# Two fused transformer layers with a 256-step recurrence: the loops over the steps written out as straight code

## What is computed

```
def step(carry, tgt):                      # 256 times, batch 4, 64 context positions
    s, c, alpha = carry
    f = conv1d(alpha, conv_w, 'SAME')      # 10 channels, 101 taps
    e = va . tanh(enc_proj + s @ Wa_s.T + f @ Wa_f.T + ba)
    alpha = softmax(where(mask, e, -1e30))
    g = sum_t alpha[t] * hbatch[t]
    y = tanh(g @ L_gy_w.T + L_gy_b + s @ L_sy.T) @ L_yy_w.T + L_yy_b
    rec = tgt @ L_ys.T + s @ L_ss.T + g @ L_gs_w.T + L_gs_b
    ig, fg, cg, og = split(rec, 4)
    c = sig(fg) * c + sig(ig) * tanh(cg)
    s = sig(og) * tanh(c)
    return (s, c, alpha), y
```

## Time and profile before

| | us |
|---|---|
| median of 3 runs | 1775.03 |
| lowest, highest | 1773.21, 1776.44 |
| profiled execution, its span from the first to the last instruction (no other time of it is listed) | 1777.0 |
| PE busy | 1506.0 |
| DVE busy | 919.2 |
| ACT busy | 528.9 |
| POOL busy | 387.5 |

### The profile page before, as it was taken

One profiled execution on the slowest core, in us unless ns is written; L12 is line 12 of the kernel. 1 busy time (PEld: TensorE's weight loads), 2 busy tenths in 40 slices (PEclk: granted clock), 3 DMA queues, 4 the chain that ended last, 5 costly groups with the idle time before them and its releaser, 6 DMA issues.

```text
span 1777.0 us, 43152 instructions
## 1 busy us (share of the span) xinstructions
PE 1506.0 (85%) x15683; PEld 1022.2 (58%) x15683; DVE 919.2 (52%) x4293; ACT 528.9 (30%) x2023; POOL 387.5 (22%) x1030
## 2 busy tenths in 40 slices
PE   6547999999888888888888888888888888887999
PEld 3334454544666666666666666666666666664443
DVE  4996643331555555555555555555555555553422
ACT  1342231221333333333333333333333333331211
POOL 3344321220000222222222222222222222222211
PEclk7658999999555555555555555555555555555999
DMA  8330000001200000000000000000000000000000
GB/s 326 141 115 11 1 1 0 1 1 52 77 0 0 0 0 0 0 0 0 0 0 0 0 0 0 0 0 0 0 0 0 0 0 0 0 0 1 1 24 25
DMA packets 17363, 34.51 MB, mean 19 GB/s; under 512 B 7476, under 2 KB 8675, under 8 KB 17332
## 3 DMA queue, kind: packets, MB, share of 16 engines
q1 hardware_dynamic: 17332, 34.10, 5.3%
HBM read 32.00 MB, written 2.10 MB: 19 GB/s over the span
## 4 chain that ended last, share of the span: by engine, by line
PE 62%; DVE 25%; issue 6%; ACT 5%; POOL 1%; DVEq 1%; SPq 1%; DMA 0%; POOLq 0%; ACTq 0%
PE bank L1243 18%; PE bank L1073 11%; PE bank L1193 6%; PE bank L1088 6%; PE bank L1221 5%; ACT eh L960 4%; DVE interT L746 4%; PE bank L1199 4%; DVE krep L764 3%; PE bank L1213 3%; DVE rinv L755 3%; DVE rs L743 2%; DVE g L760 2%; PE bank L1231 2%; DVE gat L771 2%
## 5 line engine op out<-in xcount | busy, mean ns | idle before, releaser
L1243 PE MATMUL bank<-krep,uh 128*128 128x128 f32 x1024 | 313.1, 461 | 23.6
L1243 PEld LDWEIGHTS bank<-krep,uh 128*128 128x128 f32 x1024 | 237.4, 320 | 92.4 <-DVE krep L764 92.4
L493 POOL TENSOR_TENSOR sscale<-ex,rinv 128x8 f32 x256 | 51.3, 200 | 667.6 <-DVE rinv L755 667.6
L1221 PE MATMUL bank<-eh,krep 128*128 128x4 f16 x2048 | 95.3, 168 | 92.5 <-ACT eh L960 92.5
L764 DVE TENSOR_TENSOR krep<-inv,ahn 128x128 f32<-128x128 f32 x512 | 162.2, 356 | 0.0
L1073 PE MATMUL bank<-xT,wbig 128*128 128x512 f16 x672 | 157.2, 386 | 3.7 <-DVE xT L591 3.7
L743 DVE TENSOR_TENSOR rs<-bank,rin 128x8 f32<-128x8 f32 x256 | 42.8, 167 | 198.1 <-PE bank L1199 198.1
L1221 PEld LDWEIGHTS bank<-eh,krep 128*128 128x128 f16 x2048 | 74.1, 105 | 114.0 <-ACT eh L960 114.0
L963 ACT ACTIVATE xs<-gat 64x8 f32<-64x8 f32 x256 | 53.4, 208 | 288.7 <-DVE gat L771 288.7
L955 ACT ACTIVATE interT<-bank 128x128 f16<-128x128 f32 x256 | 71.2, 278 | 216.9 <-PE bank L1193 216.9
L1181 PE MATMUL bank<-enc,identb 128*128 128x128 bf16 x771 | 128.4, 303 | 0.0
(11 more groups left out here) (201 smaller groups left out, 3044.5 us busy)
## 6 DMA issues: line engine op xcount, KB each, us to landing
wbig<-d_gate_qT SPq DMA_DIRECT2D x4, 896.0 KB, 10.1
wbig<-d_up_qT SPq DMA_DIRECT2D x4, 896.0 KB, 20.7
wbig<-d_down_qT SPq DMA_DIRECT2D x1, 3584.0 KB, 30.5
d_out<-x_sb SPq DMA_DIRECT2D x8, 256.0 KB, 2.0
sscale<-d_gate_sT SPq DMA_DIRECT2D x2, 896.0 KB, 8.6
interT<-d_gate_sT SPq DMA_DIRECT2D x2, 896.0 KB, 14.9
sscale<-d_up_sT SPq DMA_DIRECT2D x2, 896.0 KB, 4.2
interT<-d_up_sT SPq DMA_DIRECT2D x2, 896.0 KB, 4.3
```

Source lines behind the costliest of these rows:

```text
L1221: ins = mm(bank[4][:, 4 * gp:4 * gp + 4], hg2[:, j, h, gp * P:(gp + 1) * P], e[:, 4 * h:4 * h + 4], start=(first and gp == 0 and j == 0 an ...
L1243: mm(bank[1 - par][:, 0:P], uh[:, h, :], qv[:, h, :, :], start=False, stop=False, skip_group_check=True)
```

## The change

All five loops (two on POOL, one each on DVE, ACT and PE) become Python loops. The 256 steps stand in the program one after the other, the registers are gone, each wait is against a constant and each slice has a constant address. The computation and the order of the working instructions on each engine stay as they were.

```diff
--- before.py
+++ after.py
@@ -487,14 +487,14 @@
                 l = i * 2 + par
 
                 pool.wait_ge(s["s_ready"], l + 1)
-                nc.gpsimd.tensor_copy(shist2[:, bass.ds(i, 1), par, :], s2[:, par:par + 1, :]).then_inc(s["kept"], 1)
+                nc.gpsimd.tensor_copy(shist2[:, i:i + 1, par, :], s2[:, par:par + 1, :]).then_inc(s["kept"], 1)
 
                 pool.wait_ge(s["rinv_ready"], l + 1)
-                nc.gpsimd.tensor_tensor(ahist2[:, bass.ds(i, 1), par, :].rearrange("p one (o b) -> p (one o) b", o=2),
+                nc.gpsimd.tensor_tensor(ahist2[:, i:i + 1, par, :].rearrange("p one (o b) -> p (one o) b", o=2),
                                         ex[:, par, :].rearrange("p (o b) -> p o b", o=2),
                                         rinv[:, par:par + 1, :].broadcast_to([P, 2, B]), ALU.mult).then_inc(s["hist_done"], 1)
 
-            with pool.Fori(0, SPLIT0) as i:
+            for i in range(SPLIT0):
                 for par in range(2):
                     keep(i, par)
             pool.wait_ge(s["w1_in"], 96)
@@ -503,19 +503,19 @@
             nc.gpsimd.memset(wscale, WSCALE).then_inc(s["split_scaled"], 1)
             nc.gpsimd.memset(piece_scaled, 0.0).then_inc(s["split_done"], 1)
             pool.wait_ge(s["split_scaled"], 1)
-            with pool.Fori(SPLIT0, S // 2) as i:
+            for i in range(SPLIT0, S // 2):
                 keep(i, 0)
 
                 piece = i - SPLIT0
                 pool.wait_ge(s["split_done"], piece + 1)
-                nc.gpsimd.tensor_tensor(piece_scaled.unsqueeze(1), piece_float[:, bass.ds(piece, 1), :],
+                nc.gpsimd.tensor_tensor(piece_scaled.unsqueeze(1), piece_float[:, piece:piece + 1, :],
                                         wscale.unsqueeze(2).broadcast_to([P, 1, PIECE]), ALU.mult).then_inc(s["split_scaled"], 1)
                 pool.wait_ge(s["split_scaled"], piece + 2)
-                nc.gpsimd.tensor_copy(piece_part[0][:, bass.ds(piece, 1), :], piece_scaled.unsqueeze(1)).then_inc(s["split_high"], 1)
+                nc.gpsimd.tensor_copy(piece_part[0][:, piece:piece + 1, :], piece_scaled.unsqueeze(1)).then_inc(s["split_high"], 1)
                 keep(i, 1)
                 pool.wait_ge(s["split_high"], piece + 1)
-                nc.gpsimd.tensor_tensor(piece_part[1][:, bass.ds(piece, 1), :], piece_scaled.unsqueeze(1),
-                                        piece_part[0][:, bass.ds(piece, 1), :], ALU.subtract).then_inc(s["split_done"], 1)
+                nc.gpsimd.tensor_tensor(piece_part[1][:, piece:piece + 1, :], piece_scaled.unsqueeze(1),
+                                        piece_part[0][:, piece:piece + 1, :], ALU.subtract).then_inc(s["split_done"], 1)
 
             def prelude(c):
                 yield
@@ -735,12 +735,12 @@
                 return ap.rearrange("p (o b) -> p o b", o=2)
 
 
-            with dve.Fori(0, S // 2) as i:
+            for i in range(S // 2):
                 for par in range(2):
                     l = i * 2 + par
 
                     dve.wait_ge(s["sp_done"], l + 1)
-                    nc.vector.tensor_tensor(rs[:].unsqueeze(1), bank[6][:, 0:8].unsqueeze(1), rin2[:, bass.ds(i, 1), par, :], ALU.add)
+                    nc.vector.tensor_tensor(rs[:].unsqueeze(1), bank[6][:, 0:8].unsqueeze(1), rin2[:, i:i + 1, par, :], ALU.add)
 
                     dve.wait_ge(s["th_full"], l + 1)
                     nc.vector.tensor_tensor(th_lo, th, th_hi, ALU.subtract).then_inc(s["th_lo_ready"], 1)
@@ -948,7 +948,7 @@
                 for _ in gates_input(1, b):
                     pass
 
-            with act.Fori(0, S // 2) as i:
+            for i in range(S // 2):
                 for par in range(2):
                     l = i * 2 + par
                     act.wait_ge(s["pre_done"], l + 1)
@@ -1183,7 +1183,7 @@
             masks()
             context_part(0)
 
-            with pe.Fori(0, S // 2) as i:
+            for i in range(S // 2):
                 for par in range(2):
                     l = i * 2 + par
```

## The result

| | before | after |
|---|---|---|
| median, lowest to highest, us | 1774.78, 1773.21 to 1776.44 (4 runs) | 1816.59, 1814.40 to 1818.01 (4 runs) |
| span of the profiled execution | 1777.0 | 1816.2 |
| DVE busy, of it L764, L778 | 919.2, 162.2, 39.5 | 933.2, 164.5, 45.0 |
| POOL busy | 387.5 | 382.1 |

The straight code is slower: the ratio of the times is 1.0228, 95% interval 1.0204 to 1.0252. Forecast were 33 us more; the measured difference of the medians is 41.8 us.

A forecast was written before the change was run, and what follows sets the result against it. The 256-step recurrence, a chain of waits of 4.526 us a step, was taken to bound the kernel. The terms, 1777+0+0+33+0=1810 us for a profiled execution, gave 1808 us as the median; the range on record was 1772 to 1830.

The forecast's parts named there:

- Part 1: Loop branches, counters and register waits on PE, ACT and DVE go: 0, as the jump falls into waiting time.
- Part 2: The address instruction before DVE's L743 goes, moving it up 0.11 us: cost 0, since L746 waits for L956.
- The rival in which L743 held L746: L746 gains what L743 gains, 256x0.11=28 us: 1747 us, faster; chance 0.07.
- Part 3, the mechanism: Without POOL's address instructions the weight-split piece starts 0.09 to 0.08 us before DVE's `q0` and stops it.
- the rival in which `q0` isn't stopped: The piece doesn't get ahead of `q0`, or `q0` isn't stopped; nothing new in the chain, 1775 us; chance 0.22.
- would still end with the piece: On DVE, if the short `gat` ahead of `q0` lost to POOL's piece, `q0` would still end with the piece.
- Part 3, the price: Piece of 368 ns; `rinv` end to `q0` end 0.76 us, now 0.61: 0.15 in 224 steps, 33 us slower.
- The literal reading of the rule of the port: All 0.28 us of `q0` falls after the end of L511: 0.28 us a step, 63 us, 1838 us.
- Part 4: Longer code, 107 more instruction packets on queue 8, hidden if fetched one ahead: 0, bounds 0 and 150 us.
- The turning point: POOL's lead over DVE's `q0` above which POOL wins, put between -0.02 and +0.06 us.
- The step from the profile to the median: The profiled execution before lies 2 us above the median of three runs (1775.03), so 1810 becomes 1808 us.

The follow-up runs named there:

- Run 1: The changed kernel with POOL's two register loops put back, PE, DVE and ACT staying straight; 1774.59 us, ratio 1.0001 to the kernel before.
- run 8: The kernel before, with its loops, with POOL's pieces of the weight split moved between L490 and L493; 1773.96 us against 1775.18, ratio 0.9989.
- run 4: The changed kernel with POOL's pieces of the weight split moved between L490 and L493; 1774.31 us, ratio 0.9998.
- run 3: The changed kernel with one more POOL wait, so that L511 and L517 wait until `q0` is written; 1774.09 us, ratio 0.9993.
- run 10: Run 4's kernel plus a one-input POOL copy of 96 columns behind L493, on an unused tile; 1797.94 us, ratio 1.0135.
- run 9: Run 4's kernel plus a write-only POOL memset of 512 columns behind L493, on an unused tile; 1773.65 us, ratio 0.9993.
- run 6: The changed kernel with L511 and L517 also waiting for `ahn` (L769), just ahead of `q0` on DVE; 1779.67 us, ratio 1.0013.
- run 5: The changed kernel with L511 and L517 also waiting for `g1` (L760) on DVE; 1821.40 us, ratio 1.0248.

## Why the prediction was right, and where a term was off

The direction, the place and the kind of the loss were as forecast, and 1816.59 us lies in the range. By its own steps:

- **Part 1, branches, counters, register waits: 0.** Right. Run 1 has all of PE, DVE and ACT straight and stands at 1.0001. With loops and without (runs 8 and 4) the recurrence differs by 0.9 us, some 0.003 a step. The mean step of 4.526 that the argument rests on contains the one long step with L501; without that it is 4.524. The Trainium skill, "Advanced Engine Details and Errata", section Control Flow Timing, had been set beside it with an estimate of 14 us less; these runs don't show that.
- **Part 2, L743 moves up 0.11 us, worth 0.** Right in both halves. L743 starts 0.245 us after L955 instead of 0.354, and L746 still 0.03 after L956. The timeline of ACT and DVE after the change shows it as the earlier trace rows do before:

```profile
921.92 0.27 ACT L956 ACTIVATE interT<-bank 128x128 f32<-128x128 f32 x1
...
921.99 0.17 DVE L743 TENSOR_TENSOR rs<-bank,rin 128x8 f32<-128x8 f32 x1 [0.78 <-PE bank L1199]
922.22 0.29 DVE L746 TENSOR_TENSOR interT<-interT 128x128 f16<-128x128 f32 x1
```

  The rival in which L743 held L746 falls with it.
- **Part 3, the mechanism.** Right: L493 starts 0.08 us after `rinv` ends (forecast 0.09), the piece 0.157 after L493 (0.15), 0.08 us ahead of `q0` (0.09 and 0.08); `q0` takes 441 and 485 ns (forecast some 430), `q1` is back at 279, and the first 31 steps are untouched. Runs 3 and 4 take only the meeting away and get everything back, which also settles the rival in which `q0` isn't stopped. `gat` did keep its place, as the forecast had it, but by only 3 to 6 ns, and that was luck. The remark that `q0` "would still end with the piece" if `gat` lost is wrong: in run 10 `gat` lost, and `q0` ended 0.22 us after the copy instead of the 0.145 of a stretched `q0`. In 224 steps these 0.075 us would, as an estimate, have been 17 us more.
- **Part 3, the price.** Here is the term that was mis-sized. "1.91 ns a column, so 200+88x1.91=368 ns for the 96 of a piece" was used for both kinds of piece. L511 takes 374 ns, near the 368, but in part by luck: its own length is 346 (run 3), and 28 ns are its wait behind `gat`, which the forecast had at nothing. L517 reads one float and one half operand and writes half; it takes 419 ns, 391 by itself, and this is where the sum falls short. With the measured lengths the forecast's own sum is 0.083+0.157+0.374+0.147=0.761 us in the even step and 0.083+0.157+0.419+0.144=0.803 in the odd one, against 0.61 before. In steps it came out as 0.146 and 0.189 us: 112x0.146+112x0.189=37.5 us, as the profiles show, where the forecast had 33. The rows had it: 0.41 for L511 and 0.52 for L517. To the nanosecond these are 413 and 515. L517 started 57 ns nearer to `q0`'s start (14 ns behind it, against 71), so 57 of the 102 ns between them were a longer wait for `q0`, and the other 45 L517's own length (391 against 346).
- **The literal reading of the rule of the port.** The Trainium skill, "SBUF — State Buffer", section Who interferes with whom, has the loser held for the whole instruction; by that the loss would have been 63 us. In its rule on which instructions meet, the runs agree: a POOL instruction that reads stops a DVE instruction with two inputs (run 10), one that only writes doesn't (run 9). In the length of the hold they don't, as far as recorded starts and ends tell it: `q0` ends 0.14 to 0.15 us after the piece's recorded end in every run in which it loses, which is half of its own 0.28. (That section of the Trainium skill has the words "for the whole instruction" where it speaks of DVE's two-port modes, and gives no length for the case of two inputs.)
- **Part 4, longer code: 0.** Right. 103 instruction packets more on queue 8, where 107 were forecast (and 54 more on queue 14, which the forecast didn't count), and the first 31 steps take 4.516 us, not more than before. The DMA queues of the page after the change (packets, MB, share):

```profile
q8 instruction: 123, 2.02, 0.5%
```

- **The turning point** was put "between -0.02 and +0.06 us of lead". The runs narrow it to between 0 and +0.02, as the last section tells.
- **The step from the profile to the median**, 2 us less. It sets a span (1777.0) against the time of a run (1775.03). A run is 1.8 us longer than its span, so 4 us had to be taken off, and the sum was 1806.
- Not forecast: the 4 us by which the medians differ beyond the recurrence.

## What to carry to other kernels

When instructions go from an engine that isn't in the chain, ask which of its working instructions start earlier by it, and what runs on DVE at that moment: a POOL instruction that reads SBUF and starts just ahead of a DVE instruction with both inputs in SBUF holds that up until shortly before its own recorded end, and if the DVE one is in the chain, nearly all of the hold is paid (`q0` 0.16 and 0.20 us longer, the steps 0.146 and 0.189). Look at the starts of single instructions around the chain, not at the groups: the mean of L764 moved by 4 ns here, and the recurrence by 38 us. And where such a meeting costs, move POOL's work into the time in which it waits anyway, behind its own semaphore if need be; but follow what else it then meets, as run 6 shows.

## What the runs showed of the hardware that wasn't expected

Who starts first by the record wins, down to some 10 ns. These are the leads of POOL over DVE: 0.08 us (changed kernel), 0.04 (run 5), 0.021 to 0.028 (L515 over `ab`, run 6), and DVE is stopped in each. With POOL 0.003 to 0.006 us behind (the piece and `gat` in the changed kernel), 0.014 behind (L517 and `q0` before the change) or 0.032 behind (run 6) it isn't. In between the record doesn't decide: the copy 0.008 to 0.014 ahead of `gat` (run 10) wins, and so does the cast L501 0.006 ahead of it; the cast L514, 0.005 to 0.006 ahead of `q1` in the changed kernel, loses. The stopped DVE instruction keeps its recorded start and only gets longer.

Neither side is held for the other's whole recorded length. A stopped DVE instruction ends after POOL's recorded end by its own length less some 0.15 us: `q0` (0.28 us alone) 0.145 after it, `gat` (0.167) 0.02 after it, and `ab` (0.16) 0.01 before it. An estimate from these lengths: DVE goes on 0.14 to 0.17 us before POOL's recorded end. The other way round, L511 and L517 before the change start 0.071 and 0.014 us behind `q0` and are 67 and 124 ns longer than by themselves (413 and 515 against 346 and 391). Both sums give 0.14 us from `q0`'s start, half of its length. Behind the short `gat` the same sum gives 0.03 us, the 28 ns of run 5's comparison.

The same can be seen at the long cast L501. Before the change it came 0.02 us after `q0`; in the changed kernel it comes 0.006 us ahead of `gat`, as the timeline of POOL and DVE in that step shows:

```profile
585.77 0.92 POOL L501 CAST wbig<-wbig 16x896 f16<-16x896 f32 x1
585.77 0.94 DVE L771 TENSOR_TENSOR gat<-g,rs 128x8 f32<-128x8 f32 x1
586.63 0.28 DVE L764 TENSOR_TENSOR krep<-inv,ahn 128x128 f32<-128x128 f32 x1
```

`gat` takes 0.94 us instead of 0.17 and `q0` comes after it; this one step costs 0.25 us more than in the kernel before.

A wait against a register costs the same as one against a constant: L746 starts 0.03 us after L956 with either. What costs is the address that is worked out from the register: the instruction for it holds the wait, and the release takes 0.15 us instead of 0.04 on DVE (L743 behind L1199) and 0.18 instead of 0.08 on POOL (L493 behind L755). In this kernel that delay kept POOL behind `q0`, and it was worth 38 us.
